# An extra full-array product ahead of every second unit of maxima, in both attentions of a two-layer transformer

## What is computed

```python
x = layernorm(x + L0_attn(x))     # causal, 16 heads of 8, RoPE, output projection
x = layernorm(x + L0_ffn(x))      # 7 routed experts (top 2) and a shared one
x = layernorm(x + L1_attn(x))     # not causal, 16 heads of 8, RoPE, no projection
x = layernorm(x + L1_ffn(x))      # dense, four layers of 512
```

## Time and profile before

| | us |
|---|---|
| median of 3 runs | 1616.12 (1610.1 to 1623.22) |
| the profiled execution | 1627.57 |
| its span, first to last instruction | 1625.9 |
| causal attention's loop, first to last reading of the outputs | 82.4 to 522.1 |
| expert feed-forward, with the ends of its neighbours | 522.1 to 830.5 |
| second attention's loop, as the first | 830.5 to 1333.4 |
| dense feed-forward | 1333.4 to 1625.9 |

### The profile page before, as it was taken

One profiled execution on the slowest core, in us unless ns is written; L12 is line 12 of the kernel. 1 busy time (PEld: TensorE's weight loads), 2 busy tenths in 40 slices (PEclk: granted clock), 3 DMA queues, 4 the chain that ended last, 5 costly groups with the idle time before them and its releaser, 6 DMA issues. The chain is left out here.

```text
span 1625.9 us, 21073 instructions
## 1 busy us (share of the span) xinstructions
PE 1321.6 (81%) x6651; PEld 681.9 (42%) x6651; DVE 927.4 (57%) x2838; ACT 795.7 (49%) x1543; POOL 520.5 (32%) x476
## 2 busy tenths in 40 slices
PE   3678977788898586983589888888888867999997
PEld 1334333333333454761223223233232216888885
DVE  3546665675563774547557777777686513343443
ACT  1234444554444662533146656557565434655653
POOL 3314423551411465654203113113030002554453
PEclk9966576875556698995557778778585557999998
DMA  4212112211200402431321121120220000000000
GB/s 98 35 22 41 19 23 40 40 19 23 40 2 1 127 7 63 109 66 34 80 56 24 17 40 18 23 40 16 26 41 1 1 0 20 1 26 13 13 19 14
DMA packets 55918, 52.77 MB, mean 32 GB/s; under 512 B 8000, under 2 KB 38720, under 8 KB 55824
## 3 DMA queue, kind: packets, MB, share of 16 engines
q1 hardware_dynamic: 51808, 48.33, 15.4%
q0 software_dynamic: 3696, 2.76, 1.3%
q10 hardware_dynamic: 320, 0.52, 0.1%
HBM read 15.74 MB, written 8.06 MB: 15 GB/s over the span
## 5 line engine op out<-in xcount | busy, mean ns | idle before, releaser
L430 ACT ACTIVATE a_prob<-a_ps_s 128x512 f32<-128x512 f32 (+1 forms) x896 | 472.3, 568 | 461.2 <-PE a_ps_s L502 458.9
L578 DVE TENSOR_REDUCE a_mx<-a_ps_m 128x1 f32<-128x512 f32 x512 | 329.3, 684 | 156.0 <-PE a_ps_m L517 154.6
L517 PE MATMUL a_ps_m<-a_kst,a_qst 24*128 24x512 f32 (+3 forms) x1024 | 379.5, 577 | 46.4 <-DMA a_qst<-a_lo_q 36.9
L502 PE MATMUL a_ps_s<-a_qst,a_kst 25*128 25x512 f32 (+3 forms) x1024 | 359.7, 572 | 49.5 <-DMA a_qst<-a_mrow 34.3
L534 PE MATMUL a_ps_o<-a_prob,a_vst 128*32 128x512 f32 (+3 forms) x2048 | 339.6, 749 | 2.2 <-POOL a_prob L368 1.4
L575 DVE CUSTOM_DVE_ANT_0 a_junk<-a_ps_m,maskw 128x384 f32<-128x384 f32 (+3 forms) x512 | 230.1, 487 | 188.0 <-PE a_ps_m L517 186.0
L502 PEld LDWEIGHTS a_ps_s<-a_qst,a_kst 25*128 25x128 f32 x1024 | 158.8, 247 | 404.9 <-ACT a_prob L430 207.2
L517 PEld LDWEIGHTS a_ps_m<-a_kst,a_qst 24*128 24x128 f32 x1024 | 169.8, 246 | 77.9 <-issue 40.5
L368 POOL TENSOR_SCALAR_AFFINE_SELECT a_prob<-a_prob 128x512 f32<-128x512 f32 x128 | 79.7, 635 | 308.7 <-ACT a_prob L430 308.4
L335 POOL TENSOR_TENSOR a_rot_k<-a_rot_k,sin_table 128x512 f32<-128x512 f32 x16 | 20.4, 1272 | 313.4 <-DVE a_rot_k L586 313.4
L480 PE MATMUL a_ps_x<-ident,a_oT 128*128 128x128 f32 x256 | 60.5, 382 | 70.4 <-ACT a_oT L438 48.4
(11 more groups left out here) (290 smaller groups left out, 1885.3 us busy)
## 6 DMA issues: line engine op xcount, KB each, us to landing
a_kst<-a_hi_k SPq DMA_DIRECT2D x128, 64.0 KB
a_qst<-a_hi_q SPq DMA_DIRECT2D x128, 64.0 KB
f_w<-in_L_ffn_W_dram SPq DMA_DIRECT2D x21, 256.0 KB, 3.5
a_kst<-a_lo_k SPq DMA_DIRECT2D x64, 64.0 KB
a_qst<-a_lo_q SPq DMA_DIRECT2D x64, 64.0 KB
x_tiles<-in_L_attn_x_dram SPq DMA_DIRECT2D x8, 256.0 KB, 4.8
normed_rows_dram<-f_nrm SPq DMA_DIRECT2D x8, 256.0 KB, 2.3
f_hT_hi<-expert_sums_dram SPq DMA_DIRECT2D x4, 512.0 KB, 6.0
```

The source lines that it names most:

```text
L430: act.activation(prob[k][:, i, 0:w], ps_s[g % SB][:, 0:w], ACT.Exp, scale=float(D) ** -0.5)\
L502: last = pe.matmul(ps_s[g % SB][:, col:col + w], kst[r][lo_row:end, t, P * j:P * j + P], qst[r][lo_row:end, t, T - w:T], start=True, stop= ...
L517: last = pe.matmul(ps_m[g % MB][:, col:col + w], qst[r][lo_row:end, t, P * j:P * j + P], kst[r][lo_row:end, t, 0:w], start=True, stop=True)
L578: ins = dve.reduce_max(out, bank[:, col:col + w], AX.X)
```

## The change

`Shapes` gets a set `warm` with the even units (0, 2, ... 10 of 12; 0, 2, ... 14 of 16). In these units `maxima` first issues one more product: the weights are all 128 rows of one 128-column block of `kst`, the moving operand all 128 rows and 512 columns of the same tile, the target is the bank of maxima. The unit's own products start a new sum in the same bank behind it and overwrite what it left in the columns that are read.

```diff
             self.large = {(0, 8): ("v", 1), (2, 8): ("xT", 2), (2, 12): ("k", 2), (3, 8): ("q", 2)}
+        self.warm = set(range(0, 12, 2)) if causal else set(range(0, 16, 2))
         self.tiles = len(self.score)
...
+                def warm(bank, r, t):
+
+                    pe.matmul(bank[:, :], kst[r][:, t, 0:P], kst[r][:, t, :], start=True, stop=True)
+
...
                     i = (i + 2) % HG
                     after(pe, s_mx, g - MB + 1)
+                    if u in sh.warm:
+                        warm(ps_m[g % MB], r, t)
                     lo_row, end = QUAD * i, QUAD * i + KROWS
```

## The result

The change makes the kernel slower: 2184.88 us (median of 4, 2184.61 to 2189.48) against 1619.67 us (median of 4), a ratio of 1.352 with a 95% interval from 1.345 to 1.360. The forecast was 1592 us with a range up to 1665 us. The profiled execution's span is 2187.8 us against 1625.9.

What follows compares the result with a forecast made beforehand. TensorE and its changing clock were taken to bound the kernel. Second attention 37 us less, causal 12 and start 2 us more: 23 us less, 1604.6 us profiled, scaled to a 1592 us median; range 1525 to 1665 us.

Steps and rivals of the forecast that it cites:

- What bounds the kernel: Both attentions: TensorE binds at the low clock; the clock is worth 6.0 us (second) and 5.6 us (causal) a step.
- the price of one extra product: Second attention 0.20 us at the high clock, 0.40 at the low; causal 0.23 and 0.50 us.
- One product's own price: One full product of 512 columns on TensorE: 0.23 us at the high clock, 0.42 us at the low.
- What it breaks: Scores and maxima no longer run together: at most another 0.23 us per extra product, 0.42 us at the low clock.
- Bounds and choice: Extra product between 0 and 0.46 us (high clock) or 0.84 us (low); a little under half chosen, the rest hidden.
- the clock's share: Time at the high clock rises from 0.38 to 0.90 in the second attention, from 0.30 to 0.60 in the causal.
- the slow step: Step at the low clock: second attention from 18.8 to 22.0 us, causal attention from 15.6 to 18.6 us.
- The sum: Second attention 37 us less, causal 12 us more, start 2 us more: 23 us less in all.
- The stops: Causal attention: TensorE's seven waits for the maxima's row, 34.3 us in total, taken as unchanged.
- The clock doesn't react: Rival, both attentions: high-clock shares stay 0.38 and 0.30, work only costs, 140 us more, 1756 us; chance 0.12.

Runs made afterwards that it cites:

- doubled products: A second extra product right behind each one of the changed kernel, 896 in all: 1832.48 us.
- single products between groups: Changed kernel with its extra products moved ahead of the odd units' scores, where no group is cut, and none ahead of the loops: 1661.19 us.
- quarter run: Changed kernel with each extra product on 24 rows, in the quarter of the unit's own maxima, instead of 128 rows: 1864.38 us.
- pairs between groups: Kernel before plus two extra products back to back ahead of the scores of units 1, 5, 9, 13, second attention alone: 1562.78 us, ratio 0.965.

## Why the prediction was wrong, point by point

**What bounds the kernel: right.** TensorE and its clock did. That the busy share doesn't tell the clock was right too: TensorE was busy 819.80 of 827.00 us at 0.50, and with doubled products 535.20 of 547.10 us at 0.97. With single products between groups the fast steps came near my guesses, 14.2 to 15.1 us for most of the second attention (14.4 forecast) and 11.2 us in the causal one (11.4). But I had forecast them for another place, so that is luck.

**The step that failed first: the price of one extra product,** in "One product's own price", "What it breaks" and "Bounds and choice". I took its columns, 0.23 us at the high and 0.42 us at the low clock, from products of one shape that follow each other, and the same again for the narrow product that it parts from its group: bounds of 0.46 and 0.84 us. But both are passages: 0.44 us at the high clock and 0.73 us at the low one. The earlier trace rows held it: the group of four took 0.44 us where one stream is 0.23, and I read it as room for four products instead of as the time that any change takes. With nothing hidden, two passages are about 0.88 and 1.45 us.

What a product cost, on steps with the same jobs: 0.86 us at the low clock in the second attention and (21.7 - 15.6) / 6 = 1.02 us in the causal one, where I had chosen 0.40 and 0.50. At the high clock the doubled products give (18.1 - 12.8) / 8 - 0.22 = 0.44 us, where I had 0.20 (an estimate). So it was twice what I chose, and at or over my upper bound at the low clock. That about half would be hidden nearly held in the second attention (0.44 of 0.88, 0.86 of 1.45); what it was the half of was too small by almost two.

**The second, and the larger in time: the clock's share,** "I take 0.90 of the time at 1.00", and 0.60 in the causal attention. The share was 0 in both. I reasoned from the extra work and left out that its passages spread the old work over more time; that this is why the clock was lost is argued. By my own slow steps, 22.0 and 18.6 us instead of 14.9 and 13.5, the share alone makes 29 x 7.1 + 29 x 5.1 = 354 us, and the rest of the way to 27.8 and 22.1 us (means of a batch) 29 x 5.8 + 29 x 3.5 = 270 us. The two failures feed each other: the doubled product pays every passage that the single one pays and is 352 us faster, with the second attention at 0.97.

**A third, smaller: the slow step.** I took 18.8 us for every step of the second attention at the low clock. In the changed kernel the step with its jobs is the shortest of a batch (25.7 against 28.0 and 29.4 us). The quarter run stood at the low clock throughout: its 657.4 us less 29 x 1.6 us of extra work leave 611 us, or 19.7 us a step, as an estimate for the kernel before at that clock.

**The sum by its own terms,** all estimates. Second attention: 827.0 - 611 = 216 us for the work at the low clock and 611 - 502.9 = 108 us for the clock, together the measured 324 us. Causal: 29 x (22.1 - 15.6) = 189 and 29 x (15.6 - 13.1) = 73 us, less the 34 us of stops for the maxima's row, which a slower TensorE swallows: 228 of 207 us. The split belongs to the low clock; the work would have cost only about 29 x (16.2 - 12.8) = 99 us at the high one.

**The stops: missed, small.** I put them at no change. In the changed kernel TensorE's waits for that row don't stand among its listed waits any more.

**The rivals.** "The clock doesn't react" had the sign, but its price of 140 us used the same wrong term, and its reason was wrong: the clock reacted, downward. None of the rivals was that the products would take the clock away. The first rival was set beside the Trainium skill, TensorE: Matmul & The Clock Gate, section Why this matters for your kernels, which asks for TensorE to be kept busy without gaps. The trace disagrees with it as a sufficient condition: TensorE was busy 819.80 of 827.00 us at 0.50.

**What was argued and not shown.** That the array is emptied at each change is my reading of 0.73 against 0.43 us; the runs show the price, not what the array does. Nor is it shown that the array's fullness is what the clock follows. The number of products per us sets the runs apart as well: in the second attention's loop 2.9 in the changed kernel, 3.7 in the quarter run (both at 0.50), 4.4 before (0.69), 4.8 with doubled products (0.97) and 5.3 with pairs between groups (0.93). It is itself lower at the low clock, and no run here tells the two readings apart.

## What to carry to other kernels

Before adding a full-array product among products that share the array by quarters, price it as a whole passage (here 0.44 us at the high clock and 0.73 us at the low, for 512 columns), add one more if it cuts a group in two, and price a second one right behind it as its columns alone (0.22 and 0.43 us). If work is to hold the clock, put it in runs, between groups and where TensorE waits for banks anyway: the same eight products a step gave 2185 us cutting groups in both attentions, 1955 us in the second alone, and 1563 us there in four pairs between groups. Even so, try it for each stage: in the causal attention, where TensorE stops in each batch, such pairs won nothing (426.2 against 427.5 us). Check a reading of the granted clock against the length of a product whose shape is known.

## What the runs showed of the hardware that I had not expected

- A full product between quarter products costs 0.73 us at the low clock for 512 columns and 0.41 us for 128, so about 0.30 us is fixed; the same product behind its like costs 0.43 us. The Trainium skill, TensorE: Matmul & The Clock Gate, section Back-to-back issue gap, gives columns / 1.2 ns between products at the low clock, 427 ns for 512. The second of a pair agrees (0.43 us), the first doesn't (0.73 us).
- More work can be faster: the second attention takes 827 us at the low clock with one extra product per second unit, and 547 us almost wholly at the high one with two (one run).
- More narrow work can go with a lost clock: with a quarter product per second unit it was 0.50 in the second attention, where it had been 0.69 (one run).
- The granted clock reads 1.00 before its first recorded change, here for 776 us, in which no product of 512 columns took under 0.62 us; behind it they take 0.39 us.
